# Rotary queries of a grouped attention: from token-major with turns to feature-major with a partition swap by DMA

## The chip, the core and the metric

One core of one Trainium2 chip runs one program: a two-layer transformer stack. The metric is device time in microseconds of one execution, the median of several runs. TensorE, VectorE, ScalarE, GpSimd and SyncE each take their own instructions strictly in program order and wait for one another through semaphores; SyncE only issues DMAs here.

## The reference

Layer 0 and layer 1 both hold an attention with rotary positions and grouped keys. What the change touches is this part (the form for head width 64; the other has `H, HK, D = (16, 4, 128)` and a sliding window of 128 keys):

```python
q = (h @ wq).reshape(B, S, NHEADS, HEAD_DIM)
k = (h @ wk).reshape(B, S, KVHEADS, HEAD_DIM)
v = (h @ wv).reshape(B, S, KVHEADS, HEAD_DIM)
...
def rot(t):
    t1, t2 = (t[..., :half], t[..., half:])
    return jnp.concatenate([-t2, t1], -1)
return (q * cos + rot(q) * sin, k * cos + rot(k) * sin)
...
scores = jnp.einsum('bqhd,bkhd->bhqk', q, k) / np.float32(np.sqrt(HEAD_DIM))
scores = jnp.where(causal[None, None], scores, jnp.float32(-1e+30))
attn = jax.nn.softmax(scores, -1)
o = jnp.einsum('bhqk,bkhd->bqhd', attn, v).reshape(B, S, NHEADS * HEAD_DIM)
x = x + o @ wo
```

Around it stand a mixture of 16 experts, an attention of head width 8 and a gated feed-forward part; the change leaves those alone. The input is 4 sequences of 512 tokens and 256 features, all in float32.

## The kernel before

`Plan.whole` (L1482) lists eight phases. Three of them are calls of `attention` (L278): phases 0 and 3 with head width 64 ("narrow", 32 query and 8 key heads, causal), phase 6 with head width 128 ("wide", 16 and 4 heads, windowed). An attention runs over 16 units (c, b): c is one of NU = 4 column chunks of the weights (QW = 512 query columns, KW = 128 of K and of V), b one of the 4 sequences. A unit has T = 4 token tiles of 128, and in each tile nk groups of KV = 4 query heads (nk = 2 narrow, 1 wide): 8 steps (t, g) narrow, 4 steps wide.

**The order is written out by hand.** `Plan` appends steps to one list, and each engine's program (`tensor_program` L1507, `scalar_program`, `vector_program`, `pool_program`, `sync_program`) walks the whole list and emits what its engine has to do for a step. So the place of a step in the list is its place in every engine's queue. `prepare` (L415) is a generator that lays out the projections and rotations of the *next* unit in 32 pieces; the main loop calls `beside()` four times a step, and each call takes one piece (narrow) or two (wide). Before the first unit of an attention, `prepare(0, 0)` runs alone, with nothing beside it but the norm of the second sequence. The last unit has no next one.

**The steps that the change touches.** Values are split in two parts, a high one rounded to fp32r and a low one, the rest; a product is then three matmuls (high x high, low x high, high x low) for each of the two halves of 256 features.

- `q_product`: TensorE multiplies the token tile (stationary) with 512 query columns, L1532 to L1534, six matmuls into one PSUM bank, tokens on the partitions.
- `q_rotate`: TensorE does the same for 256 columns of K and V. VectorE takes the query bank times cosine (L1965, 512 columns) and its swapped halves times sine (L1967, L1968, 256 columns each). Halves of a head lie side by side in the free dimension there.
- `v_copy` (ScalarE, L1802) and `k_rotate`: VectorE rotates K; GpSimd adds the two products of the queries (L2336) and of K (L2342) into the tile `tm`.
- `q_turn`: TensorE turns four 128x128 blocks of `tm` (L1540) so that features are on the partitions; ScalarE writes the high part (L1806); `q_low`: VectorE writes the low part (L1973).
- `k_turn` and `k_low` do that for K (L1546, L1810, L1978).

In a step the list then holds: the first scores (L1559), the weighing of V by the probabilities of two steps ago (L1577, in odd steps), the normalisation of the step before (L1994, L1997), a piece, the exponentials (L1816), the low part of the weighed values (L2002), the projection out (L1589 to L1591, result added at L2006) in even steps, a piece, the other scores, the turns of the probabilities of the step before (L1568, copied at L1821) for the first two key tiles, the exponentials, a piece, the turns for key tiles 2 and 3, a piece. A maximum is L1988.

SyncE: `fetch` loads weights into two staging tiles, `clear` (L2559) writes zeros to the DRAM buffer `sorted`, two DMAs of 2304 KB at the start of each of eight units of a narrow attention (c = 1 and 2).

## Time and profile before

| | us |
|---|---|
| median of 3 runs | 3728.14 |
| lowest, highest of them | 3719.02, 3735.12 |
| span of the profiled execution, first to last instruction | 3687.3 |

No time of its own is listed for the profiled execution; its span is 40.8 us under the median of the runs, and that is taken as what lies around the span.

How to read the profile: the page gives each engine's busy share; the windows give it for a stretch, with the clock granted to TensorE (1.00 is its upper level of 2.4 GHz, 0.50 the lower of 1.2); the timeline lists instructions with start and duration, several of the same group merged in one row; a group's row has count, busy time in total and the mean of one in ns. PE is TensorE, DVE VectorE, ACT ScalarE, POOL GpSimd, SP SyncE. In the windows, PE durations are those of single pipelined matmuls, so that the distance from start to start tells what one costs. Narrow attentions lie at about 20 to 900 and 1710 to 2590 us of the span, the wide one at about 3000 to 3600.

### The profile page before, as it was taken

To read this page: it belongs to the slowest core of one execution; us is meant where nothing else is said; L and a number is where in the kernel's file an instruction comes from. 1 tells how busy PE (TensorE), PEld (TensorE's weight loads), DVE (VectorE), ACT (ScalarE), POOL (GpSimd) and SP (SyncE) were. 2 spreads that over 40 slices of the span, in tenths; PEclk is the share of its full clock that TensorE was granted. 3 is DMA by queue.
4 is the path that set the end of the run, shared out by engine and by line. 5 is a ranking of instruction groups with operands and counts; after the bars stand their busy time and mean duration, and the time that the engine had idled before them with its cause. 6 is when DMAs were issued, how large, how long until landed. Compare 5 with 4: busy or idle time off the path is not lost. (4 is left out here: it accounts for less than half of the span.)

```text
span 3687.3 us, 65201 instructions
## 1 busy us (share of the span) xinstructions
PE 3303.7 (90%) x22154; PEld 2194.8 (60%) x22154; DVE 2631.0 (71%) x8703; ACT 1933.5 (52%) x5275; POOL 990.3 (27%) x960
## 2 busy tenths in 40 slices
PE   6999999987997899997899999988799749999975
PEld 4666767664554344445667667665455437887853
DVE  5888888885444788873788888887344567777755
ACT  4667767664222366774676767666222125555531
POOL 3211112233454001012121212143444332222213
PEclk8999999998998689997999999998899769999986
DMA  4140500013755322302060500011756300000010
GB/s 129 52 170 7 166 1 1 20 48 110 178 91 116 70 46 58 73 23 72 1 220 1 172 1 1 4 48 57 215 88 122 89 1 15 1 16 4 1 34 23
DMA packets 202239, 234.78 MB, mean 64 GB/s; under 512 B 20662, under 2 KB 188536, under 8 KB 201080
## 3 DMA queue, kind: packets, MB, share of 16 engines
q1 hardware_dynamic: 170968, 190.48, 17.0%
q0 software_dynamic: 30944, 40.14, 6.5%
q8 instruction: 181, 2.97, 0.3%
q14 instruction: 146, 1.20, 0.1%
HBM read 98.13 MB, written 133.73 MB: 63 GB/s over the span
## 5 line engine op out<-in xcount | busy, mean ns | idle before, releaser
L1816 ACT ACTIVATE p_prob<-bank,p_small 128x256 f32<-128x256 f32 (+3 forms) x1280 | 646.2, 515 | 156.0 <-DVE p_small L1988 151.3
L1988 DVE CUSTOM_DVE_ANT_0 bank<-bank,p_mask 128x256 f32<-128x256 f32 (+3 forms) x1280 | 579.0, 490 | 97.1 <-PE bank L1559 85.7
L2336 POOL TENSOR_TENSOR p_tm<-p_rope_a,p_rope_b 128x512 f32<-128x512 f32 x192 | 245.8, 1280 | 1269.0 <-DVE p_rope_b L1968 1264.5
L1559 PE MATMUL bank<-p_k,p_q 64*128 64x256 f32 (+3 forms) x3840 | 529.2, 347 | 13.6 <-ACT p_prob L1816 12.5
L1821 ACT ACTIVATE p_prT<-bank 128x512 f32<-128x512 f32 x752 | 426.0, 601 | 211.5 <-PE bank L1568 209.6
L1568 PE MATMUL bank<-g_ident,p_prob 128*128 128x128 f32 x3008 | 438.3, 284 | 54.4 <-DVE p_prob L1997 20.8
L1997 DVE TENSOR_SCALAR p_prob<-p_prob,p_small 128x256 f32<-128x256 f32 (+3 forms) x1280 | 424.5, 395 | 11.3
L1577 PE MATMUL bank<-p_prT,p_v 128*64 128x512 f32 (+1 forms) x1504 | 428.2, 619 | 0.3 <-ACT p_prT L1821 0.3
L1568 PEld LDWEIGHTS bank<-g_ident,p_prob 128*128 128x128 f32 x3008 | 330.0, 142 | 150.6 <-issue 50.2
L1559 PEld LDWEIGHTS bank<-p_k,p_q 64*128 64x128 f32 (+1 forms) x3840 | 339.1, 188 | 116.1 <-issue 65.1
L2034 DVE TENSOR_REDUCE p_nmax<-bank 128x1 f32<-128x512 f32 x512 | 320.8, 683 | 56.8 <-PE bank L1618 54.6
L1844 ACT ACTIVATE p_prT<-bank 128x512 f32<-128x512 f32 x512 | 278.1, 597 | 132.1 <-PE bank L1630 129.7
L1751 PE MATMUL bank<-p_w,p_hT 128*128 (+1 forms) x632 | 325.7, 598 | 0.1
L1532 PE MATMUL bank<-p_w_hi,p_aT_hi 128*128 128x512 f32 (+1 forms) x768 | 287.5, 374 | 5.5 <-DVE p_aT_lo L1930 4.6
L1816 ACT ACTIVATION_READ_ACCUMULATOR p_prob<-bank,p_small 128x1 f32 x1280 | 267.3, 209 | 0.0
L1533 PE MATMUL bank<-p_w_hi,p_aT_lo 128*128 128x512 f32 (+1 forms) x768 | 266.4, 347 | 0.0
L1534 PE MATMUL bank<-p_w_lo,p_aT_hi 128*128 128x512 f32 (+1 forms) x768 | 265.9, 346 | 0.0
L1825 ACT ACTIVATE p_oT_hi<-bank 128x512 fp32r<-128x512 f32 x192 | 114.8, 598 | 242.1 <-PE bank L1577 240.3
L1589 PE MATMUL bank<-p_o_hi,p_oT_hi 128*128 128x256 f32 x768 | 226.4, 295 | 5.8 <-DVE p_oT_lo L2002 5.8
L1965 DVE TENSOR_TENSOR p_rope_a<-bank,p_cos 128x512 f32<-128x512 f32 (+1 forms) x384 | 186.7, 486 | 62.4 <-PE bank L1534 60.8
L1577 PEld LDWEIGHTS bank<-p_prT,p_v 128*64 128x64 f32 (+1 forms) x1504 | 126.7, 148 | 169.4 <-issue 161.1
L1590 PE MATMUL bank<-p_o_hi,p_oT_lo 128*128 128x256 f32 x768 | 216.7, 282 | 0.0
(288 smaller groups left out, 6215.8 us busy)
## 6 DMA issues: line engine op xcount, KB each, us to landing
sorted<-p_blank SPq DMA_DIRECT2D x32, 2304.0 KB, 19.2
p_w<-in_L_ffn_w SPq DMA_DIRECT2D x96, 256.0 KB, 4.5
p_h_in<-sorted SPq DMA_DIRECT2D x158, 144.0 KB, 2.7
p_k_st<-k_saved SPq DMA_DIRECT2D x16, 288.0 KB
p_q_st<-q_saved SPq DMA_DIRECT2D x16, 288.0 KB
g_stage<-in_L_ffn_wq SPq DMA_DIRECT2D x8, 512.0 KB, 3.8
g_stage<-in_L_ffn_wo SPq DMA_DIRECT2D x16, 256.0 KB, 4.3
q_saved<-p_qp SPq DMA_DIRECT2D x16, 256.0 KB, 3.2
```

Source lines behind the costliest of these rows:

```text
L1532: pe.matmul(use.ap[:, 0:n], hi, whi[:, k, cols(c0, n)], start=k == 0, stop=False)
L1533: pe.matmul(use.ap[:, 0:n], lo, whi[:, k, cols(c0, n)], start=False, stop=False)
L1559: ins = pe.matmul(h.use.ap[:, 0:n], q[rows, at, :], k[rows, kp, o.g, keys], start=i == 0, stop=i == 2)
L1568: ins = pe.transpose(s.use.ap[:, j * P:(j + 1) * P], o.probs[j].ap[:, s.kt * P:(s.kt + 1) * P], ident[:, :])
L1577: ins = pe.matmul(s.use.ap[cols(o.g * A.hd, A.hd), :], o.u.v.ap[:, o.k0 + kt, cols(o.g * A.hd, A.hd)], o.prT[kt].ap, start=kt == 0, stop=k ...
L1751: ins = pe.matmul(o.up.ap, o.hT.ap[:, k * P:(k + 1) * P], w_all(A)[:, bass.ds(at + k * 2 * H, 2 * H)], start=k == 0, stop=k == KC - 1)
L1816: act.activation(s.prob.ap[:, 0:s.o.w], s.use.ap[:, 0:s.o.w], ACT.Exp, bias=sm[:, 0, j:j + 1], scale=-1.0, accum_out=sm[:, 1, j:j + 1]).th ...
L1821: act.activation(s.prT.ap, s.use.ap, ACT.Copy).then_inc(s.use.free[0].sem)
L1844: act.activation(s.pt.ap, s.use.ap, ACT.Exp).then_inc(s.use.free[0].sem)
L1988: dve.tensor_tensor_reduce(x, x, A.mask[:, A.mask.shape[1] - o.w:], -1.0, FAR, ALU.add, ALU.min, o.sm.ap[:, 0, h.j:h.j + 1]).then_inc(made)
L1997: dve.tensor_scalar(o.probs[j].ap[:, 0:o.w], o.probs[j].ap[:, 0:o.w], o.sm.ap[:, 2, j:j + 1], None, ALU.mult).then_inc(made)
L2034: dve.tensor_reduce(A.nmax[:, s.qt % 2, s.t, s.r, s.g % 2:s.g % 2 + 1], s.use.ap, axis=AX.X, op=ALU.max, negate=True).then_inc(s.use.free[ ...
```

## The change

The queries are projected with the features on the partitions: the weight columns are stationary and 256 tokens move (`q_product`, now one of 4 x 2 blocks of 128 features x 256 tokens per unit, HS = 256). VectorE multiplies the block by turned tables `cosT` and `sinT` (128 x 512, made once per attention by the step `rope_tables`: three copies on GpSimd, eight turns on TensorE, two copies on ScalarE). The other half of a head now lies on other partitions, 32 away (narrow) or 64 away (wide), so SyncE moves the sine product between partitions with 4 (narrow) or 2 (wide) DMAs of 32 or 64 partitions x 1 KB each into `q_swap`, of which there is one buffer (`q_cos` and `q_sin` have two). `q_sum`: GpSimd adds. `q_parts`: ScalarE writes the high and VectorE the low part straight into the query tile. There are no turns of queries. V, K and the scores are computed as before; `v_copy`, `k_rotate` and K's low part get places of their own in the list. The 32 pieces of `prepare` are laid out anew by `pieces_of`. The query tiles become three of 256 tokens (before five of 128), `tm` one tile of K alone, and the two staging tiles get fixed users (one for Q, K and V, one for the output weights).

```diff
-        mem = [top(f"stage{i}", [P, 1536]) for i in range(2)]
-        self.stage = Ring([m[:, :] for m in mem])
+        self.stage = [Ring([top(f"stage{i}", [P, n])[:, :]]) for i, n in enumerate((1536, KV * D))]
...
-        rope_a = Ring([sb(f"rope_a{i}", [P, QW + KW])[:, :] for i in range(2)])
-        rope_b = Ring([sb(f"rope_b{i}", [P, QW + KW])[:, :] for i in range(1)])
-        tm = Ring([sb(f"tm{i}", [P, QW + nk * P])[:, :] for i in range(2)])
+        A.cosT, A.sinT = sb("cosT", [P, S]), sb("sinT", [P, S])
+        rope_a = Ring([sb(f"rope_a{i}", [P, KW])[:, :] for i in range(2)])
+        rope_b = Ring([sb(f"rope_b{i}", [P, KW])[:, :] for i in range(1)])
+        tm = Ring([sb(f"tm{i}", [P, nk * P])[:, :] for i in range(1)])
+        turned_cos = Ring([sb(f"q_cos{i}", [P, HS])[:, :] for i in range(2)])
+        turned_sin = Ring([sb(f"q_sin{i}", [P, HS])[:, :] for i in range(2)])
+        swapped = Ring([sb(f"q_swap{i}", [P, HS])[:, :] for i in range(1)])
+        swap_count = self.count(f"p{ph}_swapped")
         v_sb = Ring([sb(f"v{i}", [P, T, KW])[:, :, :] for i in range(3)])
-        q_st = Ring([sb(f"q{i}", [P, 8, P], F32R)[:, :, :] for i in range(5)])
+        q_st = Ring([sb(f"q{i}", [P, 2, KV, HS], F32R)[:, :, :, :] for i in range(3)])
...
-            rotated = {}
-            for t in range(T + 1):
-                if t < T:
-                    yield from products_of(c, b, unit, t, rotated)
-                if t:
-                    yield from turned_of(unit, t - 1, rotated[t - 1])
-
-        def products_of(c, b, unit, t, rotated):
+            yield from pieces_of(c, b, unit)
+
+        def rope_tables():
+            s = self.step("rope_tables", A)
+            s.twice = [x.ap.rearrange("p (t n) -> p t n", t=T) for x in prT.slots[0:2]]
+            s.uses = [wring.take() for _ in range(2)]
+            s.spread = [self.pool_made.up() for _ in range(3)]
+            for x, use in zip(prT.slots, s.uses):
+                x.users.append(use.full)
+            return [use.free for use in s.uses]
+
+        def q_product(c, b, unit, i, h):
             s = self.step("q_product", A)
+            s.c, s.b, s.i, s.h, s.use, s.ready = c, b, i, h, wring.take(), [aT_ready[b], w_ready[c]]
+            if i == 0:
+                unit.q.append(q_st.take())
+            s.q, s.cos, s.sin, s.swap = unit.q[h], turned_cos.take(), turned_sin.take(), swapped.take()
+            s.count = swap_count
+            s.swapped = swap_count.up(16 * 2 * P // A.hd)
+            w_used[c] = s.use.full
+            s.sin.users.append(s.swapped)
+            return s
+
+        def q_sum(x):
+            s = self.step("q_sum", A)
+            s.x, s.made = x, self.pool_made.up()
+            x.swap.users.append(s.made)
+            x.summed = s.made
+
+        def q_parts(unit, x):
+            s = self.step("q_parts", A)
+            s.x, s.hi_made, s.lo_made = x, self.scalar_made.up(), self.vector_made.up()
+            x.cos.users.append(s.lo_made)
+            if x.i == KV - 1:
+                unit.q_made += [s.lo_made] * 2
+
+        def kv_product(c, b, unit, t):
+            s = self.step("kv_product", A)
             s.c, s.b, s.t, s.use, s.ready = c, b, t, wring.take(), [aT_ready[b], w_ready[c]]
-            qb = s.use
-            yield
-            s = self.step("q_rotate", A)
-            s.c, s.b, s.t, s.qb, s.kb, s.ready = c, b, t, qb, wring.take(), [aT_ready[b], w_ready[c]]
+            w_used[c] = s.use.full
+            s.v, s.v_made = unit.v, self.scalar_made.up()
+            unit.v_made.append(s.v_made)
+            return s
+
+        def k_rotate(x):
+            s = self.step("k_rotate", A)
+            s.t, s.use, s.v_made = x.t, x.use, x.v_made
             s.ra, s.rb, s.tm = rope_a.take(), rope_b.take(), tm.take()
-            kb = s.kb
-            w_used[c] = kb.full
-            v = self.step("v_copy", A)
-            v.t, v.kb, v.v, v.made = t, kb, unit.v, self.scalar_made.up()
-            unit.v_made.append(v.made)
-            yield
-            k = self.step("k_rotate", A)
-            k.t, k.kb, k.qb, k.ra, k.rb, k.tm, k.v_made = t, kb, qb, s.ra, s.rb, s.tm, v.made
-            k.q_sum, k.k_sum = self.pool_made.up(), self.pool_made.up()
-            s.ra.users.append(k.k_sum)
-            s.rb.users.append(k.k_sum)
-            rotated[t] = s.tm, k.k_sum
-            yield
-            yield
-
-        def turned_of(unit, t, rotated):
-            s = self.step("q_turn", A)
-            s.tm, s.ready = rotated
-            s.use, s.q = wring.take(), q_st.take()
-            s.hi_made = self.scalar_made.up()
-            lo = self.step("q_low", A)
-            lo.use, lo.q, lo.hi_made = s.use, s.q, s.hi_made
-            yield
+            s.k_sum = self.pool_made.up()
+            s.ra.users.append(s.k_sum)
+            s.rb.users.append(s.k_sum)
+            return s
+
+        def k_turn(unit, x):
             k = self.step("k_turn", A)
-            k.t, k.tm, k.use, k.k, k.hi_made = t, s.tm, wring.take(), unit.k, self.scalar_made.up()
-            s.tm.users.append(k.use.full)
-            lo = self.step("k_low", A)
-            lo.t, lo.use, lo.k, lo.hi_made = t, k.use, unit.k, k.hi_made
-            unit.q.append(s.q)
-            unit.q_made.append(s.use.free)
+            k.t, k.tm, k.ready, k.use, k.k, k.hi_made = x.t, x.tm, x.k_sum, wring.take(), unit.k, self.scalar_made.up()
+            x.tm.users.append(k.use.full)
             unit.k_made.append(k.use.free)
-            yield
-            yield
-            yield
+
+        def pieces_of(c, b, unit):
+            last = None
+            for t in range(T):
+                h, i = t // 2, t % 2 * 2
+                x = q_product(c, b, unit, i, h)
+                yield
+                kv = kv_product(c, b, unit, t)
+                yield
+                k = k_rotate(kv)
+                yield
+                if last:
+                    q_parts(unit, last)
+                q_sum(x)
+                yield
+                last = q_product(c, b, unit, i + 1, h)
+                yield
+                k_turn(unit, k)
+                yield
+                yield
+                q_parts(unit, x)
+                q_sum(last)
+                yield
+            q_parts(unit, last)
...
+        A.turned_tables = rope_tables()
...
+        elif s.kind == "q_product":
+            whi = A.w_hi[:, s.c % 2, :].rearrange("p (k n) -> p k n", k=KC)
+            wlo = A.w_lo[:, s.c % 2, :].rearrange("p (k n) -> p k n", k=KC)
+            tok, part, out = cols(s.h * HS, HS), cols(s.i * P, P), s.use.ap[:, 0:HS]
+            w.wait_ge(s.use.before, *s.ready)
+            for k in range(KC):
+                hi, lo = A.aT_hi[:, s.b, k, tok], A.aT_lo[:, s.b, k, tok]
+                pe.matmul(out, whi[:, k, part], hi, start=k == 0, stop=False)
+                pe.matmul(out, whi[:, k, part], lo, start=False, stop=False)
+                ins = pe.matmul(out, wlo[:, k, part], hi, start=False, stop=k == KC - 1)
+            ins.then_inc(s.use.full[0].sem)
...
-        elif s.kind == "q_turn":
...
-            for j in range(QW // P):
-                ins = pe.transpose(s.use.ap[:, j * P:(j + 1) * P], s.tm.ap[:, j * P:(j + 1) * P], ident[:, :])
-            ins.then_inc(s.use.full[0].sem)
...
+        elif s.kind == "q_parts":
+            x = s.x
+            w.wait_ge(x.summed, x.q.after)
+            act.activation(x.q.ap[:, 0, x.i, :], x.cos.ap, ACT.Copy).then_inc(made)
...
+        elif s.kind == "q_product":
+            tok, x = cols(s.h * HS, HS), s.use.ap[:, 0:HS]
+            w.wait_ge(s.use.full, *A.turned_tables, s.cos.after)
+            dve.tensor_tensor(s.cos.ap, x, A.cosT[:, tok], ALU.mult)
+            w.wait_ge(s.sin.after)
+            dve.tensor_tensor(s.sin.ap, x, A.sinT[:, tok], ALU.mult).then_inc(s.use.free[0].sem)
+
+        elif s.kind == "q_parts":
+            x = s.x
+            w.wait_ge(s.hi_made, x.q.after)
+            dve.tensor_tensor(x.q.ap[:, 1, x.i, :], x.cos.ap, x.q.ap[:, 0, x.i, :].bitcast(F32), ALU.subtract).then_inc(made)
...
-        elif s.kind == "q_low":
-            x = s.use.ap.rearrange("p (j n) -> p j n", j=QW // P)
-            w.wait_ge(s.hi_made, s.q.after)
-            dve.tensor_tensor(s.q.ap[:, 4:8, :], x, s.q.ap[:, 0:4, :].bitcast(F32), ALU.subtract).then_inc(s.use.free[0].sem)
...
+        elif s.kind == "q_sum":
+            x = s.x
+            w.wait_ge(x.use.free, x.swapped, own.turn())
+            pool.tensor_tensor(x.cos.ap, x.cos.ap, x.swap.ap, ALU.add).then_inc(made)
...
+        elif s.kind == "q_product":
+            hf = A.hd // 2
+            w.wait_ge(s.use.free, s.swap.after)
+            for j in range(P // hf):
+                sp.dma_start(s.swap.ap[cols(j * hf, hf), :], s.sin.ap[cols((j ^ 1) * hf, hf), :]).then_inc(s.count.sem, 16)
```

Two places of the new order. First VectorE at the end of a narrow unit (t = 3 of one unit, then t = 0 of the next; L1988, now L2050, is a maximum over scores, L1994, now L2056, the start of the normalisation). Before:

```order
L1973 TENSOR_TENSOR p_q<-bank,p_q 128x512 [waits scalar_made]
L2002 TENSOR_TENSOR p_oT_lo<-bank,p_oT_hi 128x512
L1978 SCALAR_TENSOR_TENSOR p_k<-bank,p_k 128x2x128 [waits scalar_made]
L1988 ISA bank,p_small<-bank,p_mask 128x512 [waits bank2_filled]
L1988 ISA p_small 128x1
L1988 ISA bank,p_small<-bank,p_mask 128x512 [waits bank3_filled]
L1988 ISA p_small 128x1
L1988 ISA bank,p_small<-bank,p_mask 128x128 [waits bank0_filled]
L1988 ISA p_small 128x1
```

And now:

```order
L2064 TENSOR_TENSOR p_oT_lo<-bank,p_oT_hi 128x512 [waits scalar_made]
L2040 SCALAR_TENSOR_TENSOR p_k<-bank,p_k 128x2x128 [waits scalar_made]
L2050 ISA bank,p_small<-bank,p_mask 128x512 [waits bank2_filled]
L2050 ISA p_small 128x1
L2050 ISA bank,p_small<-bank,p_mask 128x512 [waits bank3_filled]
L2050 ISA p_small 128x1
L2019 TENSOR_TENSOR p_q<-p_q_cos,p_q 128x256 [waits scalar_made] x2
L2050 ISA bank,p_small<-bank,p_mask 128x128 [waits bank0_filled]
L2050 ISA p_small 128x1
L2050 ISA bank,p_small<-bank,p_mask 128x128 [waits bank1_filled]
```

Ahead of the first piece stood the low part of the queries (L1973), now L2014, the sine product, has that place. The low part (L2019) is now the last thing of the step, twice at a unit's end, behind the maxima of the old step and ahead of those of the next; each waits for ScalarE.

Second SyncE, at the fifth unit of the first attention. Before, eight of the first attention's seventeen clears in one row among the fetches:

```order
L2453 DMA g_stage0<-in_L0_ffn_wq 128x2x512
L2453 DMA g_stage0<-in_L0_ffn_wk 128x2x128
L2453 DMA g_stage0<-in_L0_ffn_wv 128x2x128
L2453 DMA g_stage1<-in_L0_ffn_wo 64x4x256 x2
L2559 DMA sorted<-p0_blank 128x16x288 x8
L2453 DMA g_stage0<-in_L0_ffn_wq 128x2x512
L2453 DMA g_stage0<-in_L0_ffn_wk 128x2x128
L2453 DMA g_stage0<-in_L0_ffn_wv 128x2x128
```

And now:

```order
L2550 DMA p0_q_swap0<-p0_q_sin1 32x256 x4
L2550 DMA p0_q_swap0<-p0_q_sin0 32x256 x4
L2550 DMA p0_q_swap0<-p0_q_sin1 32x256 x4
L2640 DMA sorted<-p0_blank 128x16x288 x2
L2550 DMA p0_q_swap0<-p0_q_sin0 32x256 x4
L2550 DMA p0_q_swap0<-p0_q_sin1 32x256 x4
L2550 DMA p0_q_swap0<-p0_q_sin0 32x256 x4
```

SyncE's swaps (L2550) stand before and behind the clears, eight groups of four a unit, and each group waits for VectorE's sine product and for GpSimd's sum of the block before.

## Rows read from the trace of the kernel before

**Rows 1.** The page: busy us of each engine, its share of the span, instructions.
```profile
PE 3303.7 (90%) x22154; PEld 2194.8 (60%) x22154; DVE 2631.0 (71%) x8703; ACT 1933.5 (52%) x5275; POOL 990.3 (27%) x960
```

**Rows 2.** Windows, a narrow and a wide stretch: span, then busy of PE, PEld, DVE, ACT, POOL.
```profile
400.00:600.00 200.00, 198.50 (x1362) 137.79 (x1359) 169.35 (x586) 140.14 (x407) 38.06 (x34) 1.00 0.07 22
3200.00:3400.00 200.00, 196.41 (x1244) 160.66 (x1243) 149.91 (x554) 108.66 (x335) 53.85 (x52) 1.00 0.03 9
```

**Rows 3.** Timeline of TensorE in two narrow units: start us, us, engine, line, what.
```profile
501.79 0.66 PE L1540 MATMUL bank<-g_ident,p_tm 128*128 128x128 f32 x4
502.28 0.38 PE L1546 MATMUL bank<-g_ident,p_tm 128*128 128x128 f32 x2
...
506.86 0.40 PE L1533 MATMUL bank<-p_w_hi,p_aT_lo 128*128 128x512 f32 x1
507.09 0.40 PE L1534 MATMUL bank<-p_w_lo,p_aT_hi 128*128 128x512 f32 x1
...
508.14 0.28 PE L1590 MATMUL bank<-p_o_hi,p_oT_lo 128*128 128x256 f32 x1
508.26 0.28 PE L1591 MATMUL bank<-p_o_lo,p_oT_hi 128*128 128x256 f32 x1
...
551.02 0.66 PE L1540 MATMUL bank<-g_ident,p_tm 128*128 128x128 f32 x4
```

**Rows 4.** Groups of instructions by form (the first is the page's): busy us, mean ns.
```profile
L1816 ACT ACTIVATE p_prob<-bank,p_small 128x256 f32<-128x256 f32 (+3 forms) x1280 | 646.2, 515 | 156.0 <-DVE p_small L1988 151.3
...
L2342 POOL TENSOR_TENSOR p_tm<-p_rope_a,p_rope_b 128x256 f32<-128x256 f32 x128 | 93.9, 733 | 32.1 <-DVE p_rope_b L1968 18.0
...
L1965 DVE TENSOR_TENSOR p_rope_a<-bank,p_cos 128x512 f32<-128x512 f32 x192 | 132.0, 688 | 61.5 <-PE bank L1534 60.8
L1973 DVE TENSOR_TENSOR p_q<-bank,p_q 128x512 fp32r<-128x512 f32 x192 | 131.6, 685 | 67.2 <-ACT p_q L1806 67.2
...
L1967 DVE TENSOR_TENSOR p_rope_b<-bank,p_sin 128x256 f32<-128x256 f32 x192 | 79.5, 414 | 9.6 <-POOL p_tm L2342 9.5
...
L1897 ACT ACTIVATE p_hT<-bank 128x256 f32<-128x256 f32 x158 | 60.6, 383 | 152.7 <-PE bank L1744 152.6
...
L1965 DVE TENSOR_TENSOR p_rope_a<-bank,p_cos 128x128 f32<-128x128 f32 x192 | 54.7, 285 | 0.8 <-ACT p_v L1802 0.8
...
L1967 DVE TENSOR_TENSOR p_rope_b<-bank,p_sin 128x64 f32<-128x64 f32 x192 | 40.9, 213 | 0.0
```

**Rows 5.** Timeline of VectorE and ScalarE at the end of a narrow unit.
```profile
505.73 0.73 DVE L1988 CUSTOM_DVE_ANT_0 bank<-bank,p_mask 128x512 f32<-128x512 f32 x1
...
506.58 0.68 ACT L1816 ACTIVATE p_prob<-bank,p_small 128x512 f32<-128x512 f32 x1
...
506.63 0.30 DVE L1988 CUSTOM_DVE_ANT_0 bank<-bank,p_mask 128x128 f32<-128x128 f32 x1
...
507.24 1.08 ACT L1821 ACTIVATE p_prT<-bank 128x512 f32<-128x512 f32 x2
```

**Rows 6.** DMA issues (KB each, median us to landing), and SyncE's timeline.
```profile
sorted<-p_blank SPq DMA_DIRECT2D x32, 2304.0 KB, 19.2
...
second_sum<-g_res SPq DMA_DIRECT2D x4, 512.0 KB, 3.2
...
p_q_st<-p_nm_p POOLq DMA_DIRECT2D x64, 8.0 KB, 1.9
...
169.26 0.47 SPq L2453 DMA_DIRECT2D g_stage<-in_L_ffn_wk  x1
...
172.67 43.32 SPq L2559 DMA_DIRECT2D sorted<-p_blank  x8
```

**Rows 7.** Timeline of TensorE at the start of the second narrow attention.
```profile
1714.60 0.80 PE L1532 MATMUL bank<-p_w_hi,p_aT_hi 128*128 128x512 f32 x1 [1.56 <-DVE p_aT_lo L1930]
...
1741.85 1.01 PE L1559 MATMUL bank<-p_k,p_q 64*128 64x256 f32 x6
```

More of the change, by code:

```diff
@@ L300, in fetch_o @@
                                 wo[c * QW + i * rows:c * QW + (i + 1) * rows, :].rearrange("(j d) n -> d j n", d=hd))
-                               for i in range(nk)])
+                               for i in range(nk)], 1)
         aT_ready, r2_read = {}, [None]
@@ L1522, in tensor_program @@
             ins.then_inc(s.use.full[0].sem)
-        elif s.kind in ("q_product", "q_rotate"):
-            use, c0, n = (s.use, 0, QW) if s.kind == "q_product" else (s.kb, QW, 2 * KW)
+        elif s.kind == "rope_tables":
+            for twice, use, made in zip(s.twice, s.uses, (s.spread[0], s.spread[-1])):
+                w.wait_ge(use.before, made)
+                for t in range(T):
+                    ins = pe.transpose(use.ap[:, cols(t * P, P)], twice[:, t, :], ident[:, :])
+                ins.then_inc(use.full[0].sem)
+        elif s.kind == "q_product":
[9 more added lines that the diff above has]
+            ins.then_inc(s.use.full[0].sem)
+        elif s.kind == "kv_product":
+            c0, n = QW, 2 * KW
             whi = A.w_hi[:, s.c % 2, :].rearrange("p (k n) -> p k n", k=KC)
@@ L1552, in tensor_program @@
             keys = cols(o.k0 * P, n)
-            q, k = o.u.q[o.t].ap, o.u.k.ap
+            q, k, tok = o.u.q[o.t // 2].ap, o.u.k.ap, cols(o.t % 2 * P, P)
             w.wait_ge(*(h.use.before for h in s.heads), *s.ready)
-            for i, (qp, kp) in enumerate(((0, 0), (4, 0), (0, 1))):
+            for i, (qp, kp) in enumerate(((0, 0), (1, 0), (0, 1))):
                 for h in s.heads:
                     rows = slice(0, P) if A.wide else cols(h.j % 2 * A.hd, A.hd)
-                    at = qp + (h.j if A.wide else (o.g * KV + h.j) // 2)
-                    ins = pe.matmul(h.use.ap[:, 0:n], q[rows, at, :], k[rows, kp, o.g, keys], start=i == 0, stop=i == 2)
+                    at = h.j if A.wide else (o.g * KV + h.j) // 2
+                    ins = pe.matmul(h.use.ap[:, 0:n], q[rows, qp, at, tok], k[rows, kp, o.g, keys], start=i == 0, stop=i == 2)
                     if i == 2:
```

104 lines of the change are left out of this document (54 added, 50 removed).

## Prediction

> **What bounds the kernel now.** I read the page first. TensorE is busy 90% of the span and VectorE 71% [rows 1]; the chain of waits on the page is spread thinly over matmul lines and names no single wait. So I went to the two engines by stage: in a steady stretch of the first attention (head width 64, "narrow" below) TensorE is busy 198.5 of 200 us at full clock, VectorE 169.4, ScalarE 140.1; in the attention of head width 128 ("wide") TensorE has 196.4 of 200 and VectorE 149.9 [rows 2]. A busy TensorE can be a pipelined one, so I looked at starts in the timeline: products of 512 columns start 0.23 us apart, of 256 columns 0.12 us apart, and from the four turns of the queries to those of K after them it is 0.49 us [rows 3]. They follow one another with hardly a gap, so TensorE is the bound there, not only busy. By the Trainium skill (Perfetto Trace Analysis, Identifying the Most-Contended Engine) matmul busy share is no good measure of the distance to the limit; the starts bear out the share in this case. One (c, b) unit of the narrow kind lasts 49.2 us, from the last turns of queries of one unit to those of the next, 501.79 to 551.02 [rows 3]. VectorE has (200 - 169.4) x 49.2 / 200 = 7.5 us of idle time in it [rows 2].
>
> **The change part by part.** 192 token tiles (3 attentions x 16 units x 4) are touched.
>
> *TensorE.* A tile's queries were 6 products of 512 columns and 4 turns. They become 12 products of 256: 12 x 0.12 against 6 x 0.23, nothing lost. The 4 turns go: 0.49 us a tile, less some 0.1 us that a further group costs at its start (estimate, half of the step from one 512 product to the next): 0.4 us a tile, 1.5 us a unit. If TensorE stayed the bound everywhere this is 45 units with a next one to prepare x 1.5 = 68 us.
>
> *VectorE's work.* Before: 688 + 2 x 414 + 685 ns a tile; after: four 256-wide products with the tables (4 x 414) and two differences of 256 columns, which now read SBUF alone; I bound these by 213 (the 64-wide row) and 414 and take 350. 2356 against 2201 [rows 4]: durations of neighbours overlap a little in the timeline, and there are six for four, so it comes out about equal. Nothing, with -0.1 and +0.2 us a tile as ends. *ScalarE:* two copies of 256 columns (383 each, [rows 4]) for one of 512, some +0.2 us on an engine with 30% free [rows 2]. *GpSimd:* two sums of 256 columns (733 each, [rows 4]) for one of 512; it is busy 38 of 200 us [rows 2]. No cost as long as nothing waits for either in order.
>
> *Something does.* This is where I put the cost. In both programs VectorE takes its instructions in order. Before, the low part of the queries (q_low) stood behind the normalisation, in the second quarter of a step. Now "q_parts" stands at the end of a step, one per step from the second to the eighth, and two at the unit's end: ScalarE makes the high part, and only then may VectorE subtract and go on to the maxima of the next scores. But at that place ScalarE is always behind. See the step end in the timeline: VectorE finishes the unit's last maximum at 505.73 + 0.73 = 506.5 and begins the next unit's scores at 506.63; ScalarE begins the last exponential at 506.58, then makes two copies of turned probabilities from 507.24 to 508.3 [rows 5]. The high part would come behind those. So VectorE waits 508.3 + 0.38 + 0.05 - 506.5, some 2.2 us, where before it went on at once and waited for the exponential (507.2) only before normalising. A step end costs: exponential 0.515 (mean of the widths), 0.1 for the accumulator's read, 0.38 for the high part (a 256-wide copy, [rows 4]) and 0.1 for two semaphores, 1.1 us; seven of them, 7.7 us. At three of the seven the rotation of K lies between (285 and twice 213, in the queue 0.46), less 1.4. Four copies of turned probabilities (ends with three or four key tiles) stand ahead, 0.54 each [rows 5], plus 2.2; the second pair at the unit's end plus 0.3. Together **8.8 us of VectorE standing still per narrow unit**. Its own work is 41.7 us a unit (169.4 x 49.2 / 200), small gaps 0.8: 51.3. TensorE would need 47.7. So VectorE, coupled to ScalarE, becomes the bound, and a unit takes about 51.2, **+2.0 us x 30 narrow units = +60 us**. Bounds: -45 us if half of the standing still falls where VectorE would have idled anyway (7.5 us are there), +110 if TensorE-heavy and VectorE-heavy steps do not even out.
>
> *Wide.* VectorE has 25% free, only one end per tile is of the bad kind (6.3 us of work + 1.5 in a step of some 8.3). TensorE's 1.5 us is partly kept: -0.8 x 15 units = -12 us (bounds -23 and +10).
>
> *The swap and its queue.* Per 128x256 block SyncE issues 4 DMAs (narrow) or 2 (wide): 1024 + 256 in all. An issue takes it 0.47 us, with the gap to the next 0.5 (a load of 128 KB; the far end are the clears, 43.3 us for 8) [rows 6]. Landing: 1.9 us for a small SBUF to SBUF transfer, the nearest row; 3.2 for 512 KB written to HBM is the far end [rows 6]. One block then needs 0.1 + 3 x 0.5 + 2.0 + 0.1 + 0.75 = 4.5 us before the next may begin, since there is one swap buffer; wide 3.5. In steady state a block comes every 6.2 us (narrow), so it fits. The tightest is the last block of a unit, which stands where the last turns of queries stood (501.79, [rows 3]): TensorE ends it near 502.6, VectorE's two products end near 503.5, the fourth DMA lands near 507.1, the sum is there at 508.0, and ScalarE wants it from 508.3 on [rows 5]: hidden, by half a microsecond.
>
> *The start of each attention is not covered.* There prepare(0, 0) runs alone; 27.2 us pass from the first product to the first scores now [rows 7]. Eight blocks one after the other through the swap: 1.3 + 0.8 + 4.5 + 7 x 4.5, then copy and difference 0.8, 39 us before the first maximum is taken; now that is the 27.2 and some 2 us for the scores: +10 us, twice; wide some +8. **+28 us** (ends 10 and 50).
>
> *Clears.* SyncE ran ahead: eight clears of `sorted` went out at 172.67 in one go, with nothing behind them that anybody waited for [rows 6]. Now they stand two by two ahead of the swaps at eight unit starts of each narrow attention. Two clears are 10.8 us of the queue at the rate of that row; SyncE can begin them some 3 us before the unit starts, so the first block is some 1 us late at worst: +8 us (0 to +60). The Trainium skill (DMA: Bandwidth & Descriptors, Queues, rings and completion order) says that on each DMA engine descriptors of a ring are consumed in order, so a swap starts only behind the clears; no row here shows a small transfer behind a clear, and my 0 to 60 is the width that this leaves.
>
> *Tables.* Three copies on GpSimd, 8 turns, 2 copies on ScalarE per attention, ahead of the first products: +3 us together (0 to 9).
>
> **Sum:** 60 - 12 + 28 + 8 + 3 = **+87 us**, 3687.3 to about 3774 of span. The median of the runs, 3728.14, is 41 us above the span, so **3815 us**. A measurement of this kernel can tell about 0.5%, 19 us, from no change.
>
> **The rivals.**
> *A, the turns pay off* (0.20). VectorE's waits at the step ends fall into idle time it has anyway; TensorE keeps setting the pace at 1.5 us less per unit. For it: TensorE 99% busy, 7.5 us of idle VectorE per unit. Against it: 8.8 us are more than 7.5, and the heavy steps (t = 3) have none of that idle time. -45 - 18 + 28 + 8 + 3 = -24, **3704 us**; it decides if the step-end waits in sum stay below some 6 us a unit. If in addition the starts cost only 10, 3685.
> *B, both cancel* (0.13): step-end waits of 7 us a unit, unit unchanged but for 0.3 us less, the starts +28: **3710 to 3747**.
> *C, the swap comes late as well* (0.17). Landing 3.2 us instead of 2.0 makes the last block 0.7 us late in 30 units (+21), each of 24 blocks at the starts 1.2 us (+29), and clears hold the first block for 4 us in 16 units (+64 against +8). +87 + 106 = **3920 us**. For it: 0.5 us of room at a unit's end, and nothing else waits so long for SyncE. Against: 1.9 us in the nearest row.
> *That the change doesn't do what it says:* the order of instructions shows no turn of queries on TensorE and four DMAs per block on SyncE; no chance of its own.
>
> **How the numbers follow.** My case 0.50, A 0.20, B 0.13, C 0.17. My case's own range is 3750 to 3870. Faster by over 0.5% (under 3709) is A with a small part of it above: 0.20; within 0.5% 0.13; slower 0.67. The range leaves out the better end of A and the worse end of C: 3695 to 3900.
>
> **What would show it.** Right: in a narrow steady stretch TensorE busy falls from 99% to some 93%, with a new wait for probabilities or banks of VectorE at its turns (L1619); VectorE's largest wait is at the difference of q_parts (L2019) for ScalarE's copy (L1863), about 8 us a unit; the unit is 51 us; first scores come 29 us or more after the first product, with GpSimd's sum (L2410) waiting for the swap. Wrong: a unit under 49 us, TensorE still at 98%, then A holds; ScalarE's copy waiting for GpSimd in steady units, then C; VectorE waiting for ScalarE less than 6 us a unit falsifies the step-end term.

## The result and the profile after

| | before | changed |
|---|---|---|
| median of 4 runs, us | 3723.97 | 4135.45 |
| lowest, highest | 3719.02, 3735.12 | 4131.11, 4141.39 |
| ratio, 95% interval | | 1.1097 [1.1071, 1.1123] |
| span of the profiled execution | 3687.3 | 4139.6 |

The forecast was slower, 3815, with a range to 3900; it is 411 us slower. Most of it lies in the attentions (405 us by the rows below). From the last difference of K of one unit to that of the next (timeline of VectorE, L1978 before, L2040 now), 15 such steps each:

| | before | changed |
|---|---|---|
| first narrow attention | 772.2 | 939.0 |
| second narrow | 772.9 | 952.8 |
| wide | 498.3 | 556.2 |
| a steady narrow unit | 49.2 | 55.6 to 66.2 |
| first product to first scores | 27.2, 27.3, 22.3 | 33.4, 36.7, 24.6 |

Windows of the changed kernel, three narrow stretches and a wide one (columns as in [rows 2], the clock granted to TensorE behind POOL):

```profile
200.00:400.00 200.00, 177.48 (x1160) 120.55 (x1159) 136.53 (x511) 116.43 (x351) 29.94 (x40) 0.94 0.23 72
400.00:600.00 200.00, 177.63 (x1135) 122.03 (x1135) 144.49 (x498) 117.15 (x344) 36.09 (x42) 0.92 0.27 90
600.00:800.00 200.00, 175.19 (x1111) 119.24 (x1110) 140.44 (x491) 116.48 (x338) 34.47 (x40) 0.91 0.30 96
3600.00:3800.00 200.00, 177.38 (x1174) 146.51 (x1172) 145.80 (x542) 101.60 (x324) 49.21 (x68) 0.98 0.18 43
```

No engine is at its limit any more: TensorE 198.5 to 177.6, VectorE 169.4 to 144.5. And in the narrow stretches the clock has fallen from 1.00 to 0.91 to 0.94: with two levels that is 2 x (0.06 + 0.08 + 0.09) x 200 = 92 of these 600 us at 1.2 GHz.

All that VectorE waited for in 400 to 600 (us in total, times, longest):

```profile
DVE p_q L2019 <- ACT p_q L1863: 39.2, 25, 2.4
DVE p_q_cos L2012 <- PE bank L1578: 9.6, 3, 3.7
DVE bank L2050 <- PE bank L1610: 6.5, 4, 2.6
```

The largest is the wait at the step end that the prediction named. One of the 25 in the timeline, with ScalarE's work and what TensorE does meanwhile and after:

```profile
521.32 0.15 DVE L2050 DVE_READ_ACCUMULATOR2_ANT p_small<- 128x1 f32 x1
...
523.79 0.43 DVE L2019 TENSOR_TENSOR p_q<-p_q_cos,p_q 128x256 fp32r<-128x256 f32 x1 [1.94 <-ACT p_q L1863]
```
```profile
521.95 0.60 ACT L1878 ACTIVATE p_prT<-bank 128x512 f32<-128x512 f32 x1 [1.45 <-PE bank L1619]
522.44 0.47 ACT L1873 ACTIVATE p_prob<-bank,p_small 128x256 f32<-128x256 f32 x1
...
523.34 0.42 ACT L1863 ACTIVATE p_q<-p_q_cos 128x256 fp32r<-128x256 f32 x1
```
```profile
520.80 1.11 PE L1619 MATMUL bank<-g_ident,p_prob 128*128 128x128 f32 x4 [0.93 <-DVE p_oT_lo L2064]
521.84 1.33 PE L1610 MATMUL bank<-p_k,p_q 64*128 64x384 f32 x6
...
523.48 0.41 PE L1577 MATMUL bank<-p_aT_lo,p_w_hi 128*128 128x256 f32 x1
...
524.36 0.28 PE L1640 MATMUL bank<-p_o_hi,p_oT_hi 128*128 128x256 f32 x1
```

VectorE has its maxima done at 521.9 and stands until ScalarE has made one turned copy, two exponentials and the high part; ScalarE itself had waited 1.45 us for TensorE's turns. TensorE's products last 0.41 us at 523.48 and 0.28 again from 524.36 at the latest. The clock says why:

```profile
516.00:520.00 4.00, 3.27 (x20) 1.94 (x18) 3.36 (x15) 2.75 (x12) 0.88 (x3) 1.00 0.12 33
520.00:524.00 4.00, 3.20 (x14) 2.44 (x15) 2.06 (x8) 2.31 (x7) 0.65 (x1) 0.59 0.12 33
520.50:521.00 0.50, 0.20 (x1) 0.20 (x2) 0.50 (x3) 0.00 (x0) 0.15 (x1) 0.72 0.00 0
521.00:522.00 1.00, 1.00 (x6) 0.67 (x5) 0.85 (x5) 0.05 (x1) 0.00 (x0) 0.50 0.09 26
524.00:528.00 4.00, 4.00 (x34) 3.61 (x34) 3.96 (x16) 1.51 (x5) 0.74 (x1) 0.98 0.00 0
```

The clock fell between 520.5 and 521, in the third of three waits of TensorE for VectorE (0.77 us before 513.68, 0.50 before 518.75, 0.93 before 520.80), and came back at about 524. So it fell before this stop of VectorE began, and TensorE was never idle during the stop: it had work, at half speed. This one stop therefore doesn't show its own price. What the rows show is that a wait of TensorE does not end with the wait, as the work behind it can run slowly for some microseconds. The price of the stops is shown by the experiments.

### The profile page after: what moved, and what is told of

The parts are those of the page before. It is cut to its first block and busy times, and to the rows that moved or that the text cites. A ratio compares the mean times of both kernels' runs of the same rounds, so it can differ in the third digit from the quotient of the medians.

```text
span 4139.6 us, 68576 instructions
## 1 busy us (share of the span) xinstructions
PE 3441.2 (83%) x22560; PEld 2288.8 (55%) x22562; DVE 2692.1 (65%) x9087; ACT 1977.9 (48%) x5473; POOL 1037.9 (25%) x1161
## 5 line engine op out<-in xcount | busy, mean ns | idle before, releaser
L1619 PE MATMUL bank<-g_ident,p_prob 128*128 128x128 f32 x3008 | 556.5, 310 | 266.6 <-DVE p_prob L2059 165.7
L2050 DVE CUSTOM_DVE_ANT_0 bank<-bank,p_mask 128x256 f32<-128x256 f32 (+3 forms) x1280 | 582.2, 488 | 103.6 <-PE bank L1610 82.4
L1619 PEld LDWEIGHTS bank<-g_ident,p_prob 128*128 128x128 f32 x3008 | 375.6, 151 | 435.1 <-DVE p_prob L2059 148.7
L2410 POOL TENSOR_TENSOR p_q_cos<-p_q_cos,p_q_swap 128x256 f32<-128x256 f32 x384 | 290.3, 756 | 1240.4 <-DMA p_q_swap<-p_q_sin 801.0
L2019 DVE TENSOR_TENSOR p_q<-p_q_cos,p_q 128x256 fp32r<-128x256 f32 x384 | 174.6, 455 | 496.0 <-ACT p_q L1863 482.4
L2059 DVE TENSOR_SCALAR p_prob<-p_prob,p_small 128x256 f32<-128x256 f32 (+3 forms) x1280 | 463.8, 426 | 11.3
L2417 POOL TENSOR_TENSOR p_tm<-p_rope_a,p_rope_b 128x256 f32<-128x256 f32 (+1 forms) x192 | 123.2, 642 | 685.3 <-DVE p_rope_b L2035 519.1
L1576 PE MATMUL bank<-p_aT_hi,p_w_hi 128*128 128x256 f32 x768 | 280.4, 365 | 4.8 <-DVE p_aT_lo L1987 4.8
L1576 PEld LDWEIGHTS bank<-p_aT_hi,p_w_hi 128*128 128x128 f32 x768 | 157.2, 205 | 156.3 <-issue 141.0
L2012 DVE TENSOR_TENSOR p_q_cos<-bank,p_cosT 128x256 f32<-128x256 f32 x384 | 160.8, 419 | 103.3 <-PE bank L1578 102.7
L1577 PE MATMUL bank<-p_aT_lo,p_w_hi 128*128 128x256 f32 x768 | 227.4, 296 | 0.0
```

Of the source, the lines that this page charges most:

```text
L1576: pe.matmul(out, whi[:, k, part], hi, start=k == 0, stop=False)
L1619: ins = pe.transpose(s.use.ap[:, j * P:(j + 1) * P], o.probs[j].ap[:, s.kt * P:(s.kt + 1) * P], ident[:, :])
L2050: dve.tensor_tensor_reduce(x, x, A.mask[:, A.mask.shape[1] - o.w:], -1.0, FAR, ALU.add, ALU.min, o.sm.ap[:, 0, h.j:h.j + 1]).then_inc(made)
L2059: dve.tensor_scalar(o.probs[j].ap[:, 0:o.w], o.probs[j].ap[:, 0:o.w], o.sm.ap[:, 2, j:j + 1], None, ALU.mult).then_inc(made)
L2410: pool.tensor_tensor(x.cos.ap, x.cos.ap, x.swap.ap, ALU.add).then_inc(made)
```

## The experiments

Ratios are to the kernel before on the same chip; chips differ (3685 to 3689 us for it on two, 3729 on two), so sizes are compared within a batch or by unit lengths.

### First batch: the place of the parts, the swap, its buffer

**e1_parts_later.** `q_parts` is put in a list and taken out one piece later, so it stands behind the next normalisation.

```
-                q_parts(unit, x)
+                late.append((unit, x))
...
                 for _ in range(pieces):
+                    parts_on()
                     next(back, None)
```

> ScalarE's high copy and VectorE's difference of each block (q_parts) move one piece later: from the end of a step to behind the normalisation of the next, where q_low stood. The swap, its queue and its one buffer are untouched. Theory M (VectorE stands at the step ends because ScalarE is behind there; the profile has 39.2 us of that wait in 200, and TensorE's half clock of 99 us in 150 to 850 follows from it): the wait of the difference for the copy falls under 2 us a unit, a narrow unit goes from 60.5 us (mean of 15) to 49 to 51, the time to 3730 to 3800. Theory C (the swap lands late and everything else only waits with it): units stay at 57 or more, the time above 4030.

3918.33, ratio 1.0513 [1.0478, 1.0549]: 217 us back, the largest single part, and yet between the two theories' numbers. (The 60.5 us a unit that the expectation starts from is not the mean of 15: that is 939.0 / 15 = 62.6, and 60.9 for the third to the thirteenth.) Units are 50.3 to 60.0 without the last two. The wait is 15.8 us in 200, not under 2 a unit:

```profile
ACT p_q L1871 <- POOL p_q_cos L2418: 19.4, 8, 8.1
DVE p_q L2027 <- ACT p_q L1871: 15.8, 8, 7.4
```

Eight long waits instead of 25 short ones, behind a ScalarE that itself waits for the sum, thus for the swap.

**e2_no_swap**, the sum reads the product with the sines unswapped.

```
-            pool.tensor_tensor(x.cos.ap, x.cos.ap, x.swap.ap, ALU.add).then_inc(made)
+            pool.tensor_tensor(x.cos.ap, x.cos.ap, x.sin.ap, ALU.add).then_inc(made)
...
-                sp.dma_start(s.swap.ap[cols(j * hf, hf), :], s.sin.ap[cols((j ^ 1) * hf, hf), :]).then_inc(s.count.sem, 16)
```

> The swap's 1280 transfers are left out: GpSimd adds the unswapped product with the sines, so the queries are not rotated rightly; the order of everything else stays as in the changed kernel. Theory M: the step ends cost what they did, only waits of ScalarE for the sum (135 us in all) and the starts (14 us longer than before) shrink: 3980 to 4060. Theory C: units of about 51 us, 3780 to 3830.

3966.61, 1.0640 [1.0611, 1.0668]: 169 us less, a little more than theory M gave. **e3_both**, both edits:

> Both edits, later parts and no swap (queries not rotated rightly): the floor of this way of making queries. Both theories: at or under the kernel before, 3660 to 3720; TensorE's 1.5 us a unit less would show as narrow units of 47.7 to 48.5 us. If it stays above 3750 a third cost is in the change (the two-column-block copies or the order of GpSimd's work).

3776.29, 1.0131 [1.0104, 1.0158]. Both theories hold beside each other: 217 for the place, then 142 for the swap. But 47 us stay against the kernel before on the same chip, where 3660 to 3720 was expected, so there is a third cost, and TensorE's saving does not show: steady units are 49.6 us. Units in which the next weights are split take 56.2 to 57.3.

**e4_two_swaps.**

```
-        swapped = Ring([sb(f"q_swap{i}", [P, HS])[:, :] for i in range(1)])
+        swapped = Ring([sb(f"q_swap{i}", [P, HS])[:, :] for i in range(2)])
```

> Two buffers for the swapped halves in place of one, each with its own count; the memory comes from one of two rope_a buffers. A swap may then start while the sum of the block before is still to come. Theory M: only the starts of the attentions and late blocks gain, 4090 to 4135. Theory C: most of the loss goes, under 3950.

4118.28, 1.1056 [1.1017, 1.1094]: 17 us, and the interval overlaps that of the change, so the total hardly tells. The starts do (28.7, 32.0, 22.3 us to the first scores, 12 us less in all). The single buffer was not it.

### Second batch: which half of the parts, the clears, the split

**e8_low_later**: the step `q_parts` is divided; ScalarE's half stays, only VectorE's moves as in e1.

```
+            s = self.step("q_high", A)
+            s.x, x.hi_made = x, self.scalar_made.up()
+            late.append((unit, x))
```

> Against the changed kernel only VectorE's difference moves one piece later, behind the next normalisation; ScalarE's high copy stays at the step's end, and the swaps stay. It splits e1's gain of 217 us. Theory M (it is VectorE's standing in its queue that costs): nearly all of it, 3900 to 3950. Rival: the copy's place in ScalarE's queue costs as much, as it holds up the exponentials when the sum is late: 4000 to 4100.

3870.83, 1.0511 [1.0486, 1.0537]; e1's kernel on a chip with nearly the same time before has 1.0589 (e9, below). By units the three attentions take 2209 us here, 2248 in e1, 2238 in e9 and 2448 in the change. The whole gain comes from VectorE no longer standing; the copy is even better left early.

**e6_clears_apart.** In the timeline of SyncE of the changed kernel, two clears go out just before a unit's first swaps, and behind it GpSimd waits for the swap:

```profile
617.17 3.77 SPq L2640 DMA_DIRECT2D sorted<-p_blank  x2
621.04 21.08 SPq L2550 DMA_DIRECT2D p_q_swap<-p_q_sin  x12
```
```profile
544.65 0.73 POOL L2417 TENSOR_TENSOR p_tm<-p_rope_a,p_rope_b 128x256 f32<-128x256 f32 x1 [5.08 <-DVE p_rope_b L2035]
546.34 0.73 POOL L2410 TENSOR_TENSOR p_q_cos<-p_q_cos,p_q_swap 128x256 f32<-128x256 f32 x1 [0.95 <-POOL p_tm L2417]
...
634.38 0.72 POOL L2410 TENSOR_TENSOR p_q_cos<-p_q_cos,p_q_swap 128x256 f32<-128x256 f32 x1 [11.67 <-DMA p_q_swap<-p_q_sin]
```

The sines of the block summed at 634.38 were ready at 620.56, 13.8 us earlier; an undisturbed block takes 3.9 (542.43 to 546.34). Of the 16 first blocks behind two clears eight took 9.1 to 11.1 us, four, with the loads of the next weights just ahead of the clears as here, 13.8 to 16.4, and four, behind the split, at most 5.5; ahead of one of these the clears went out 11 us before the swap (428.29 and 439.64). The edit, inside the steps:

```
+                clears = {1: 2 * (n_u - NU), 5: 2 * (n_u - NU) + 1, 7: E if n_u == 3 * B - 1 else None}
...
+                if clears.get(n_step) is not None:
+                    self.clear(A, clears[n_step])
```

> e1_parts_later with the clears spread: in place of two at the start of a unit, one behind the first swap of the second step and one behind that of the sixth. In e1 the units with clears (fifth to twelfth) are 0 to 8.5 us, in sum 36 us an attention, longer than those of e3_both without swaps. Theory K (two clears in a row, which keep a swap 10 to 14 us on its way instead of 3.9, are what is left of the swap's cost): 72 us less at best, 3850 to 3880. Rival (the clears' bytes disturb the swaps wherever they stand): 3900 to 3930.

3843.14, 1.0437 [1.0411, 1.0463]. Against e9's ratio that is 56 us (28 against e1's, so the ratios tell little here); the narrow attentions of the traces of e9 and of this run differ by 1701 - 1647 = 54, and the units with clears and no split are 49.3 to 50.5 us, before 52.3 to 60.5. Theory K. The rule of the Trainium skill that the prediction cited (DMA: Bandwidth & Descriptors, Queues, rings and completion order: descriptors of a ring are consumed in order) fits these rows; that it is the cause, and not the shared bandwidth, no run separates.

**e5_split_moved**, on e3:

```
+                if b == 2 and c + 1 < NU and n_step < 2:
+                    (split_qkv, split_o)[n_step](c + 1, (slot_qkv, slot_o)[n_step])
```

> e3_both (later parts, no swap, queries not rotated rightly) with the splitting of the next weights moved from the start of a unit behind the first piece of its first and second step. In e3 such a unit takes 56.5 us and its neighbours 49.6; at the split VectorE's difference takes 2.52 and 1.46 us instead of 0.42, while GpSimd subtracts the weights. Theory S (the split collides with VectorE's work on SBUF and with ScalarE's copies, and the new order has put both at one place): these units fall to 50 to 52, 3715 to 3745. Rival (the split costs what it costs wherever it stands, it was hidden before by TensorE being the bound): units stay at 55 or more, above 3765.

3749.58, 1.0174 [1.0147, 1.0201], on another chip than e3, between the two expectations: the split units are 54.3 to 55.7, little better. Moving it only changes what it collides with. **e7_all**, with e1's, e4's, e5's and e6's edits:

> The whole function, with later parts, clears apart, the split moved and two swap buffers. If the gains of the single edits add up (217, 50 to 70, 40 to 60, 15): 3770 to 3815, still slower than before; if the late swaps were worth less once they have room, 3815 to 3880.

3815.36, 1.0350 [1.0320, 1.0381]. The ranges had been set for a chip with 3729 us before; there this ratio is 3860, so the single gains did not add up in full.

### Third batch: what TensorE and VectorE were worth

**e9_parts_again:**

> e1_parts_later once more, beside the next three on one chip: the two chips so far gave the kernel before 3729 and 3685 us. 1.051 of the kernel before, as in e1, or up to 1.06 if the part outside the attentions is what differs between chips and weighs differently in the two.

3905.98, 1.0589 [1.0563, 1.0615]. The same kernel has 1.0513 on another chip: 0.8% of a ratio between batches means nothing here. It comes from the kernel before, which differs by 1.1% between these two chips while e1's differs by 0.3%.

**e10_best**, e7 with e8's edit in place of e1's:

> e7_all with only VectorE's difference later and ScalarE's copy at the step's end (as in e8_low_later). The attentions of e8 are 39 us shorter in sum than those of e1. Expected: 1.020 to 1.032 of the kernel before, below e7's 1.035.

3782.63, 1.0259 [1.0240, 1.0277], as expected; steady narrow units 49.2 to 50.1 us.

**e12_low_pool:**

```
+            pool.tensor_tensor(x.q.ap[:, 1, x.i, :], x.cos.ap, x.q.ap[:, 0, x.i, :].bitcast(F32), ALU.subtract).then_inc(made)
```

> e10_best with the low part of the queries made by GpSimd at the same place in its own queue: VectorE loses eight differences of 0.42 us a unit, 3.4 us. Theory L (with TensorE no longer setting the pace, a unit is a chain through VectorE, ScalarE and TensorE, and what is taken from VectorE shortens it): narrow units from 50 to 47 to 48.5, 1.000 to 1.015 of the kernel before. Rival (GpSimd's work on SBUF slows VectorE's as the split does, or its queue delays the next sums): 1.03 or more.

4129.31, 1.1209 [1.1185, 1.1233], as bad as the change itself; the rival's 1.03 or more came, but by another wait. Theory L wasn't tested, because this new wait came first: VectorE's next product needs the buffer that GpSimd's difference still reads.

```profile
DVE p_q_cos L2026 <- POOL p_q L2419: 31.2, 13, 4.9
```

**e11_turns_twice**, the kernel before with

```
-            for j in range(QW // P):
+            for j in [*range(QW // P)] * 2:
```

> The kernel before with each turn of the queries issued twice into the same place (same result). It asks what the turns were worth there. Theory T (TensorE sets the pace in the kernel before, as its starts without gaps say): 4 x 0.109 us more in each of 192 tiles, 84 us at most, 70 to 84 us slower than before, narrow units of 50.9 us. Rival (TensorE and the chain through the others bind equally, and the turns lie in slack): under 30 us.

3740.37, 1.0161 [1.0132, 1.0189]. Narrow units are 50.9, as theory T says; with the wide ones (34.1 for 32.9) it is 53 us by units, less than my 70, as the first and last units and the wide attention give only part. So TensorE did set the pace before: 1.7 us more of turns made a narrow unit 1.7 us longer there. That the unit shortens as much when they are taken away doesn't follow; e3's 49.6 us say it does not.

### Fourth batch: the split

In the changed kernel the four normalisations that take 1.67 us at 557.38 take 7.00 while GpSimd subtracts the weights, and TensorE waits for them:

```profile
431.91 7.00 DVE L2059 TENSOR_SCALAR p_prob<-p_prob,p_small 128x512 f32<-128x512 f32 x4
```
```profile
432.32 3.42 POOL L2368 TENSOR_TENSOR p_w_lo<-g_stage,p_w_hi 128x1536 fp32r<-128x1536 f32 x1 [1.91 <-ACT p_w_hi L1840]
435.89 2.34 POOL L2368 TENSOR_TENSOR p_o_lo<-g_stage,p_o_hi 128x1024 fp32r<-128x1024 f32 x1
```
```profile
436.09 0.48 PE L1619 MATMUL bank<-g_ident,p_prob 128*128 128x128 f32 x1 [3.25 <-DVE p_prob L2059]
438.56 0.87 PE L1619 MATMUL bank<-g_ident,p_prob 128*128 128x128 f32 x2 [2.00 <-DVE p_prob L2059]
```

The kernel before has a milder case (four such normalisations take 0.93 us at 374.49 in the same unit), and its unit was 49.2 all the same:

```profile
366.61 3.20 DVE L1997 TENSOR_SCALAR p_prob<-p_prob,p_small 128x128 f32<-128x128 f32 x4
```

**e13_chunks**, on e10:

```
+            for c in range(0, n, 256) if n >= 1024 else [0]:
+                part = slice(c, c + 256) if n >= 1024 else slice(None)
+                ins = pool.tensor_tensor(s.lo[:, part], s.raw[:, part], s.hi[:, part].bitcast(F32), ALU.subtract)
```

> e10_best with GpSimd's subtraction of the next weights in pieces of 256 columns (six and four instructions in place of one of 1536 and one of 1024 columns). In e3 and e5 a difference of VectorE that reads SBUF alone took 2.5 to 2.8 us instead of 0.42 and ended with GpSimd's instruction. Theory P (VectorE's SBUF work waits for the end of a GpSimd instruction, so a shorter one frees it sooner): no difference above 1.1 us at a split, split units of narrow attentions down from 54 to 55.7 to 51 to 53, the time 15 to 35 us under e10. Rival (both share a rate, whatever the length, or ScalarE's copies are the cost): within 8 us of e10.

**e15_best_again**, its reference:

> e10_best once more as the reference of the two others on their chip: 1.018 to 1.028 of the kernel before.

3784.17 (1.0158 [1.0127, 1.0188]) against 3802.47 (1.0195 [1.0154, 1.0235]). The medians are 18 us apart with intervals that overlap a little; the units leave no doubt: the six narrow split units go from 53.9 to 55.5 down to 49.7 to 50.0, a normal unit, 29 us in all. The longest difference of the low parts of the queries (ns min/median/max), e15 and e13:

```profile
L2033 DVE TENSOR_TENSOR p_q<-p_q_cos,p_q x384: 407/418/3190, 34.5 to 3646.4; 128x256 fp32r<-128x256 f32 x192
```
```profile
L2033 DVE TENSOR_TENSOR p_q<-p_q_cos,p_q x384: 407/418/972, 35.9 to 3622.8; 128x256 fp32r<-128x256 f32 x192
```

One of them in e15, with GpSimd's subtraction and VectorE's instructions that read a PSUM bank:

```profile
375.58 3.44 POOL L2382 TENSOR_TENSOR p_w_lo<-g_stage,p_w_hi 128x1536 fp32r<-128x1536 f32 x1 [1.91 <-ACT p_w_hi L1854]
```
```profile
375.79 0.41 DVE L2082 TENSOR_TENSOR g_res<-bank,g_res 128x256 f32<-128x256 f32 x1
376.12 3.18 DVE L2033 TENSOR_TENSOR p_q<-p_q_cos,p_q 128x256 fp32r<-128x256 f32 x1
```

Theory P holds: GpSimd ends at 379.02, the difference at 379.30, and the instruction on a PSUM bank beside it keeps its 0.41; these differences, and the normalisations above, stand until the running GpSimd instruction ends. Not every VectorE instruction on SBUF does: a reciprocal beside GpSimd's subtraction kept its 0.17 us (366.40 in the kernel before). The Trainium skill (SBUF — State Buffer, Who interferes with whom) says the two share ports under an exclusive lock that is held for a whole instruction, for VectorE instructions with two SBUF inputs or in certain modes; these traces agree, 0.42 becoming 3.19 us.

**e14_split_vector:**

```
+                dve.tensor_tensor(s.lo, s.raw, s.hi.bitcast(F32), ALU.subtract).then_inc(made)
```

> e10_best with the low part of the next weights made by VectorE itself, no GpSimd work there. Theory P: a 1536 and a 1024 column difference at 1.35 ns a column add 3.5 us to VectorE's chain and no stretching: split units 53 to 54. If ScalarE's two copies of 2.6 us are the cost, 55 to 57.

3803.90, 1.0203 [1.0174, 1.0232]. Narrow split units 52.0 to 54.3: VectorE's two instructions last 1.75 and 1.22 us, and the units are 3.3 us longer than the steady 49.8 in the mean, about that length. ScalarE's copies aren't the cost. Wide split units stay at 38 to 43 for 33 in all of these kernels. In e13 TensorE waits there for GpSimd's sum of K, up to 3.1 us, and that wait was not tried by itself.

No version beats the kernel before; of those that compute the whole function e13 comes nearest, 55 us behind it.

## Why the prediction was wrong

**The direction was right, by the named mechanism.** "VectorE standing still" at the step ends was forecast at 8.8 us a unit and is 39.2 x 60.9 / 200 = 11.9. e8, which takes that one wait away, shows it to be the largest cost. Rival A falls with it.

**The step that failed is the next one: what the wait costs.** "Its own work is 41.7 us a unit, small gaps 0.8: 51.3" lets the 7.5 us of idle time vanish in the new wait. They did not: VectorE idles (200 - 144.5) x 60.9 / 200 = 16.9 us a unit now, 11.9 for ScalarE and 4.9 for TensorE. The waits for TensorE come at other points of the chain and add. TensorE's clock is lower too (92 of 600 us at half speed; with only VectorE's wait taken away, e8, the same three windows have 0.97, 0.96, 0.97, thus 40). The prediction had no term for the clock. Taking the wait away (e1) gave 181 us less in the narrow attentions by units, 6 us a unit, where I had 2.0 net. That is three times my term.

**VectorE's own work was put at nothing** (-0.1 to +0.2 us a tile) and 41.7 us a unit was taken for the changed kernel. In e13, whose steady units have hardly a wait for ScalarE left (0.7 us in 200) and the full clock, it is more:

```profile
400.00:600.00 200.00, 192.15 (x1382) 135.26 (x1379) 173.28 (x612) 140.02 (x420) 45.08 (x59) 1.00 0.38 123
```

That is 173.28 x 49.8 / 200 = 43.1 us a unit, some 1.5 more than before (the 2356 against 2201 ns a tile of the prediction's own sum are already 0.6), and TensorE's 192.15 are 47.8, the 47.7 of the prediction. With 43.1 of work, 5.7 for which VectorE still waits for TensorE and small gaps, the unit is a little longer than the 49.2 of before. TensorE's saving was there as work and bought no time.

**Clears: 8 us forecast, 55 measured**, near my end of 60. "SyncE can begin them some 3 us before the unit starts, so the first block is some 1 us late at worst" failed: behind two clears a block took up to 16.4 us, not 4.5. The other part of rival C, a late swap in steady units, did not come: the swap took 3.9 us, and with the buffer's release a block takes 4.59 us from one sum to the next (515.34 to 519.93, GpSimd's timeline); 4.5 was forecast.

**GpSimd's queue was left out.** I costed its sums at nothing and never asked what it does beside VectorE. The new order put the split's subtraction onto VectorE's SBUF work: six narrow units of 5 us (e15 against e13), and 7 in e3. The rows of before had it, 3.20 us for four small normalisations. It was mild because of the order there: beside the subtraction of 1536 columns (362.11 to 365.59) VectorE only had instructions that read PSUM banks, and only the one of 1024 columns met the normalisations. That the rest was hidden by TensorE being the bound is argued, not shown.

**Starts: 28 us forecast, 6.2 + 9.4 + 2.3 = 18 measured**, inside 10 to 50. e4 shows that the single buffer is most of it.

**Wide: -12 forecast, +58 measured.** "TensorE's 1.5 us is partly kept" failed: 33.6 us a steady unit in e3, without swaps, against 32.9. The rest is the same waits (19 us, the change to e1), the swap's 13 us (e1 to e3), and the split units.

**Span and median.** The 41 us between the span and the median of before do not lie around the span: every run since has 1.8 us there. The chips differ by about that much, so the profile shown was probably taken on a quicker one. It did not change the verdict, but some 3776, not 3815, would have been the sum on that chip.

What stays open: the only trace of the kernel before is, by its span, from a quicker chip than the one e3 ran on, so the rests cannot be split exactly. Against the trace of before e3's attentions are 87 us longer, by the medians on one chip only 47. Of those 87 the narrow split units hold some 45, and e13 ends these; the rest, and what e13 is behind, lies in the starts, the first and last two units of the narrow attentions, the wide split units and about 0.5 us in each steady unit, and was not taken apart. In the last two units a part can be seen: the sum of a block stands behind eight DMAs that GpSimd issues itself (sines ready at 864.00, sum at 878.62), in the changed kernel

```profile
868.41 1.24 POOL L2486 DMA_INDIRECT sorted<-p_row,p_n_tiles  x1 [0.18 <-issue]
...
877.64 0.96 POOL L2486 DMA_INDIRECT sorted<-p_row,p_n_tiles  x1 [0.30 <-issue]
878.62 0.73 POOL L2410 TENSOR_TENSOR p_q_cos<-p_q_cos,p_q_swap 128x256 f32<-128x256 f32 x1
```

and the kernel before has such a row of eight as well (715.50 to 725.58), in units of 61 us. How much of each wait is the wait and how much the clock behind it was read from windows only, not isolated.

## What to carry to other kernels

An engine that sets the pace hides the stumbles of all others; before taking work off it, list those stumbles (stretched instructions, short waits), since each comes due once it no longer does. A wait put into an in-order queue is priced by adding it to the idle time that is there, unless a row shows that the two fall together. A small transfer that somebody now waits for must not share a queue with large ones that go out just ahead of it: put those behind it, apart. And place the consumer of another engine's result behind work that already had to wait for that engine.

## What the hardware showed that I had not expected

A VectorE instruction of 0.42 us on SBUF took up to 3.19 beside one GpSimd instruction, four normalisations 7.00 instead of 1.67; the same subtraction in pieces of 256 columns left no such difference over 0.97. VectorE's instructions that read a PSUM bank kept their 0.41 beside GpSimd's. Waits of TensorE of 0.77, 0.50 and 0.93 us within 8 us came ahead of more than 3 us at half clock (a mean of 0.59 in the window 520 to 524). And the kernel before differs by 1.2% between chips (3685 and 3729 us), while e1's kernel differs by 0.3% and e10's by 0.5%: a ratio to another kernel is not the same on every chip.
